# Attention scores in 64-row tiles of TensorE: two passes on opposite halves of the array

## What is computed

```python
q, k, v = split(x @ Wqkv.T + bqkv)              # 16 heads of 16
scores = einsum('bhqd,bhkd->bhqk', q, k) * hd ** -0.5
scores = where(causal, -inf, scores)            # query sees keys up to itself
attn = softmax(scores)
out = einsum('bhqk,bhkd->bhqd', attn, v)
```

## Time and profile before

| | before |
|---|---|
| median of the runs | 489.26 us |
| profiled execution, span | 490.0 us |
| TensorE busy | 400.7 us (82%) |
| VectorE busy | 327.5 us (67%) |
| ScalarE busy | 224.3 us (46%) |
| GpSimd busy | 233.4 us (48%) |
| granted TensorE clock, mean | 0.956 of full |

### The profile page before, as it was taken

How to read it: one execution, slowest core, us unless ns; L and a number is a source line. 1 busy time by engine, 2 the same in 40 slices (tenths; PEclk the granted TensorE clock), 3 DMA queues, 4 the chain that set the end, 5 groups by cost and what they waited for, 6 DMA issues and landing times.

```text
span 490.0 us, 8489 instructions
## 1 busy us (share of the span) xinstructions
PE 400.7 (82%) x2960; PEld 227.4 (46%) x2960; DVE 327.5 (67%) x619; ACT 224.3 (46%) x385; POOL 233.4 (48%) x267
## 2 busy tenths in 40 slices
PE   3737779899988999789987893887368999999980
PEld 3214335444554465443435351545145666666650
DVE  3779899558969878995688369968544444444540
ACT  2512325676556757476854761664522222232220
POOL 1482843653258622762258336347430545565542
PEclk9979999999999999899998999899859999999996
DMA  8464155726600663111222111609491344332320
GB/s 268 153 161 85 51 107 121 254 81 174 157 0 10 160 151 98 43 49 34 86 88 88 44 35 57 209 13 351 155 288 58 64 76 85 60 52 40 55 30 0
DMA packets 41319, 50.12 MB, mean 102 GB/s; under 512 B 5336, under 2 KB 36444, under 8 KB 41280
## 3 DMA queue, kind: packets, MB, share of 16 engines
q1 hardware_dynamic: 36096, 42.34, 30.3%
q0 software_dynamic: 5184, 7.25, 7.3%
HBM read 33.75 MB, written 16.75 MB: 103 GB/s over the span
## 4 chain that ended last, share of the span: by engine, by line
PE 48%; DVE 16%; POOL 7%; ACT 6%; issue 6%; DMA 5%; another core or an unknown queue 2%; SPq 0%; DVEq 0%; POOLq 0%; ACTq 0%
PE bank L1340 27%; PE bank L1454 5%; PE bank L1438 5%; PE bank L1410 3%; DVE W L1114 3%; DVE mx L1025 2%; DVE x_sb L1069 2%; PE bank L1671 2%; DMA out<-h2T,row 2%; POOL W L660 2%; ACT W L812 1%; ACT W L859 1%; PE bank L1412 1%; DVE W L1067 1%
## 5 line engine op out<-in xcount | busy, mean ns | idle before, releaser
L812 ACT ACTIVATE W<-bank 128x512 f32<-128x512 f32 (+1 forms) x176 | 95.0, 563 | 63.5 <-PE bank L1438 62.0
L1025 DVE TENSOR_REDUCE mx<-bank 128x1 f32<-128x384 f32 (+3 forms) x176 | 104.9, 633 | 23.1 <-PE bank L1412 22.6
L1340 PE MATMUL bank<-W 128*128 128x256 f16 (+2 forms) x756 | 107.4, 295 | 12.6 <-POOL W L654 3.3
L1340 PEld LDWEIGHTS bank<-W 128*128 128x128 f16 x756 | 73.9, 100 | 46.4 <-issue 12.4
L679 POOL TENSOR_SCALAR_AFFINE_SELECT W<-W 128x512 f32<-128x512 f32 x64 | 43.8, 687 | 83.3 <-ACT W L812 83.3
L1410 PE MATMUL bank<-W 126*128 126x128 f16 (+3 forms) x256 | 64.8, 308 | 14.5 <-DMA W<-qk_d 7.7
L1340 PE MATMUL bank<-W,h2T 128*128 x276 | 68.4, 385 | 3.3 <-DVE h2T L1297 2.6
L756 POOL DMA_INDIRECT out<-h2T,row x23 | 36.4, 1582 | 60.1 <-DVE h2T L1309 29.7
L1438 PE MATMUL bank<-W 128*128 128x512 f16 (+3 forms) x256 | 62.4, 305 | 2.7 <-ACT W L812 2.0
L1454 PE MATMUL bank<-W 128*32 128x128 f32 (+3 forms) x512 | 47.6, 445 | 3.1 <-POOL W L679 3.1
L1340 PE MATMUL bank<-h2T,W 128*128 128x512 f16 x192 | 44.6, 385 | 5.2 <-DVE W L1129 5.2
(11 more groups left out here) (154 smaller groups left out, 558.3 us busy)
## 6 DMA issues: line engine op xcount, KB each, us to landing
stage<-in_gup SPq DMA_DIRECT2D x14, 512.0 KB
qk_d<-W SPq DMA_DIRECT2D x48, 128.0 KB
W<-qk_d SPq DMA_DIRECT2D x32, 192.0 KB, 4.6
stage<-in_down SPq DMA_DIRECT2D x7, 512.0 KB
row<-xs_d SPq DMA_DIRECT2D x23, 130.0 KB, 5.2
xs_d<-fillb SPq DMA_DIRECT2D x2, 1040.0 KB, 5.2
x_sb<-in_x SPq DMA_DIRECT2D x4, 512.0 KB, 9.0
out<-x_sb SPq DMA_DIRECT2D x4, 512.0 KB, 4.4
```

The lines of the kernel that those rows point to most:

```text
L812: a.activation(PT[j][:, i:i + m, :], t_bank(N)[:, 0:m * w].rearrange("p (i n) -> p i n", i=m), ACT.Exp).then_inc(s_exp, 1)
L1025: v.tensor_reduce(mx_v[:, b % 2, hp0 // 4, par, i:i + m, t], SB[N % 3][:, 0:m * w].rearrange("p (i n) -> p i n", i=m), AX.X, ALU.max).then ...
L1340: i = t_.matmul(outp, l, r, start=(n == 0), stop=(n == len(prods) - 1), **kw)
```

## The change

- `scores` works on the heads of the other parity (`other_heads`), so that in each pair of units the second pass is on one half of the partitions and the first pass on the other.
- Matmuls of both passes contract only the partitions of their head: 48 rows (64 times parity onwards) in the first pass, 50 in the second. `qs` needs no second column range and no zeros; the memsets of L604 and L1167 go, and the semaphore that told of them is renamed.
- The rows of the maxima stand at partitions 48 and 49, and 112 and 113.
- The mask becomes two matmuls over 64 rows, 64 key columns of each head at a time, with selection matrices `pick` and a 64-column `maskb`. Row 63 of `maskb` masks everything, and `pick` sends it to the queries of the upper half. The columns in sum are the same.
- `constants` builds these with 18 more GpSimd instructions, most of them waiting for the one before.

```diff
+def other_heads(g):
+    return 1 - g % 2, 4 * (g // 2)

-            qs.append(early(NH * S, F16).rearrange("p (h two n) -> p h two n", two=2, n=S))
+            qs.append(early(NH // 2 * S, F16).rearrange("p (h n) -> p h n", n=S))
+            at[0] += NH // 2 * S

 def stacks(b, f):
-                if b == 0 and f == 0:
-                    sp.wait_ge(s_zero, 1)
-                if b == 1 and f == 0:
-                    sp.wait_ge(s_const, 4)
-                    sp.wait_ge(s_zero, 2)
+                if b < 2 and f == 0:
+                    sp.wait_ge(s_ones, b + 1)
-                    for a, dst in ((0, qs[r][:, :, par]), (1, ks[r])):
+                    for a, dst in ((0, qs[r]), (1, ks[r])):

 def maxima(b, f):
-                    sp.dma_start(qs[r][P - 2:P, 4 * f:4 * f + 4, par], src[par]).then_inc(s_ng[r][f], 16)
+                    p0 = 64 * par + 3 * HD
+                    sp.dma_start(qs[r][p0:p0 + 2, 4 * f:4 * f + 4], src[par]).then_inc(s_ng[r][f], 16)

 def constants():
-                link(g.tensor_copy(identb[:, :], ident[:, :]))
-                link(g.memset(maskb[:, :], 0.0))
-                g.affine_select(out=maskb[:, :], ...).then_inc(s_const, 1)
+                link(g.memset(pick[:, :, :], 0.0))
+                for lo in (0, P // 2):
+                    rows = slice(lo, lo + P // 2)
+                    link(g.memset(maskb[rows, :], 0.0))
+                    link(g.affine_select(out=maskb[rows, :], ... fill=NEG, base=0, pattern=[[-1, P // 2]], ...))
+                    link(g.affine_select(out=maskb[rows, :], ... fill=NEG, base=-(P // 2 - 1), pattern=[[0, P // 2]], ...))
+                    for part, half in ((0, 0), (1, 0), (1, 1)):
+                        link(g.affine_select(out=sel, ... fill=1.0, base=0, pattern=[[-1, P // 2]], ...))
+                    for part, half, value in ((0, 0, 0.0), (1, 0, 1.0), (1, 1, 0.0)):
+                        link(g.affine_select(out=sel, ... fill=value, base=-(P // 2 - 1), ...))
+                g.tensor_copy(ve1[0:1, 0:1], ve1[0:1, 0:1]).then_inc(s_const, 1)
...
-                g.memset(qs[1].rearrange("p h two n -> p (h two n)").bitcast(F32), 0.0).then_inc(s_const, 1)

 VectorE, before its loop
-            v.memset(qs[0].rearrange("p h two n -> p (h two n)").bitcast(F32), 0.0)

 def maxima(N) on VectorE, and def scores(N)
-                par, hp0 = group_heads(gr)
+                par, hp0 = other_heads(gr)

 def scores(N)
-                    t_.matmul(bk[:, w * i:w * (i + 1)], qs[r][0:P - 2, hp, par, P * t:w],
-                              ks[r][0:P - 2, hp, 0:w], start=(i == 0), stop=False, ...)
-                t_.matmul(bk[...][:, :, w - P:w], identb[:, :], maskb[...], start=False, stop=True, ...)
+                    p0 = 64 * par
+                    t_.matmul(bk[:, w * i:w * (i + 1)], qs[r][p0:p0 + 3 * HD, hp, P * t:w],
+                              ks[r][p0:p0 + 3 * HD, hp, 0:w], start=(i == 0), stop=False, ...)
+                rows = slice(64 * par, 64 * par + 64)
+                for part in range(2):
+                    c = w - P + 64 * part
+                    q = t_.matmul(bk[...][:, :, c:c + 64], pick[rows, part, :], maskb[rows, :]...,
+                                  start=False, stop=(part == 1), ...)

 def scores_t(N)
-                    q = t_.matmul(..., ks[r][:, hp, P * j:P * (j + 1)], qs[r][:, hp, par, P * j:S], ...)
+                    rows = slice(64 * par, 64 * par + 3 * HD + 2)
+                    q = t_.matmul(..., ks[r][rows, hp, P * j:P * (j + 1)], qs[r][rows, hp, P * j:S], ...)
```

More of the change, by code:

```diff
@@ L260, in build @@
         s_col = sem("s_col")
-        s_zero = sem("s_zero")
+        s_ones = sem("s_ones")
         s_mp = sem("s_mp")
@@ L593, in constants @@
             def constants():
-                link(g.tensor_copy(identb[:, :], ident[:, :]))
-                link(g.memset(maskb[:, :], 0.0))
-                g.affine_select(out=maskb[:, :], in_=maskb[:, :], compare_op=ALU.is_ge, fill=NEG,
-                                base=0, pattern=[[-1, P]], channel_multiplier=1).then_inc(s_const, 1)
+                link(g.memset(pick[:, :, :], 0.0))
+                for lo in (0, P // 2):
+                    rows = slice(lo, lo + P // 2)
+                    link(g.memset(maskb[rows, :], 0.0))
+                    link(g.affine_select(out=maskb[rows, :], in_=maskb[rows, :], compare_op=ALU.is_ge, fill=NEG,
+                                         base=0, pattern=[[-1, P // 2]], channel_multiplier=1))
+                    link(g.affine_select(out=maskb[rows, :], in_=maskb[rows, :], compare_op=ALU.not_equal, fill=NEG,
+                                         base=-(P // 2 - 1), pattern=[[0, P // 2]], channel_multiplier=1))
+                    for part, half in ((0, 0), (1, 0), (1, 1)):
+                        sel = pick[rows, part, 64 * half:64 * half + 64]
+                        link(g.affine_select(out=sel, in_=sel, compare_op=ALU.not_equal, fill=1.0,
+                                             base=0, pattern=[[-1, P // 2]], channel_multiplier=1))
+                    for part, half, value in ((0, 0, 0.0), (1, 0, 1.0), (1, 1, 0.0)):
+                        sel = pick[rows, part, 64 * half:64 * half + 64]
+                        link(g.affine_select(out=sel, in_=sel, compare_op=ALU.not_equal, fill=value,
+                                             base=-(P // 2 - 1), pattern=[[0, P // 2]], channel_multiplier=1))
+                g.tensor_copy(ve1[0:1, 0:1], ve1[0:1, 0:1]).then_inc(s_const, 1)
                 po.wait_ge(s_const, 2)
@@ L1409, in scores @@
                     hp = hp0 + i0 + i
-                    t_.matmul(bk[:, w * i:w * (i + 1)], qs[r][0:P - 2, hp, par, P * t:w],
-                              ks[r][0:P - 2, hp, 0:w], start=(i == 0), stop=False, skip_group_check=True)
-                t_.matmul(bk[:, 0:m * w].rearrange("p (i n) -> p i n", i=m)[:, :, w - P:w], identb[:, :],
-                          maskb[:, :].unsqueeze(1).to_broadcast([P, m, P]), start=False, stop=True,
-                          skip_group_check=True).then_inc(s_s1, 1)
+                    p0 = 64 * par
+                    t_.matmul(bk[:, w * i:w * (i + 1)], qs[r][p0:p0 + 3 * HD, hp, P * t:w],
+                              ks[r][p0:p0 + 3 * HD, hp, 0:w], start=(i == 0), stop=False, skip_group_check=True)
+                rows = slice(64 * par, 64 * par + 64)
+                for part in range(2):
+                    c = w - P + 64 * part
+                    q = t_.matmul(bk[:, 0:m * w].rearrange("p (i n) -> p i n", i=m)[:, :, c:c + 64],
+                                  pick[rows, part, :], maskb[rows, :].unsqueeze(1).to_broadcast([64, m, 64]),
+                                  start=False, stop=(part == 1), skip_group_check=True)
+                q.then_inc(s_s1, 1)
             def max_turn(b, f):
@@ L1437, in scores_t @@
                     hp = hp0 + i0 + i
-                    q = t_.matmul(t_bank(N)[:, w * i:w * (i + 1)], ks[r][:, hp, P * j:P * (j + 1)],
-                                  qs[r][:, hp, par, P * j:S], start=True, stop=True)
+                    rows = slice(64 * par, 64 * par + 3 * HD + 2)
+                    q = t_.matmul(t_bank(N)[:, w * i:w * (i + 1)], ks[r][rows, hp, P * j:P * (j + 1)],
+                                  qs[r][rows, hp, P * j:S], start=True, stop=True)
                 q.then_inc(s_st, 1)
```

13 lines of the change are left out of this document (6 added, 7 removed).

## The result

| | before | after |
|---|---|---|
| median of 16 runs each | 489.13 us | 499.86 us |
| lowest and highest | 487.86, 490.90 | 489.36, 506.72 |
| profiled execution, span | 490.0 us | 498.1 us |
| granted TensorE clock, mean of it | 0.956 | 0.900 |

The medians of all 16 runs lie 10.7 us or 2.2% apart. The ratio of undisturbed runs alone (those within 1.5% of the kernel's fastest, 6 of the 16 after, with a median of 492.9 us) is 1.0066, with a 95% interval of 1.0044 to 1.0087. So the loss is some 3 us in the quickest runs and nearer 11 in the middle of the spread, where the profiled execution lies. The forecast was 482, with a range to 496.

The account below looks back on a forecast made before the run. TensorE was taken to bound stage 0, with VectorE next and close in stages 1 and 2. Gains of 4.5, 1.7 and 2.3 us less 1.1 lost make 7.4: 490.0 to 482.6, forecast 482, range 475 to 496.

Parts of the forecast that it names:

- Overlap works: Both passes, stages 0 to 2: array halves work at once, a group takes 3.03 us, not 5.18, before deductions.
- 0.29 us a group: Taken off the overlap's 2.15 us because first-pass units start only with the last second-pass matmul ahead; leaves 1.86 us.
- no overlap: Rival: the halves don't run at once but the switches of form are paid; 494.7 us, chance 0.20.
- slow loads: Rival: loads of 64-row weights aren't hidden, 5.3 us a group, all of the gain; 495 to 500 us, chance 0.08.
- Changes of form: TensorE, between full-form jobs and the passes' row tiles: 129 more changes at 0.09 us, 11.7 us raw over all stages.
- Stage -1: First pass alone: VectorE sets the stage's length, so TensorE's 1.6 us of switches cost only 0.1 us.
- Stage 0: 7.1 us saved by overlap, less 1.8 of switches, is 5.3; 4.5 after VectorE and ScalarE take some.
- the next engine holds the pace: Rival: only stage 0 gains, 4.5 us less 1.1 and some wait; 486 to 488 us, chance 0.16.
- Stage 1: Overlap saves 2.9 us on the chain, less 1.2 of switches: 1.7 us gained.
- Stage 2: 5.0 us saved less 1.3 of switches is 3.7; cut to 2.3 since VectorE has only 5.3 us idle.
- Stage 3: No second lane to overlap; 40% of 2.6 us of switches, 1.0 us lost.
- The last sentence of the prediction: A fall of the granted clock in a stage that had 1.00 or 0.97 would make the forecast wrong; no chance given.

Follow-up runs that it names:

- twins on the other half: Changed kernel with stage -1 score matmuls (but the last few) issued again on the idle half, result unused, then mask matmuls too: 500.27 us, then 499.99 us.
- the doubles: Late-mask hybrid with every second-pass matmul of stages 0 to 2 issued twice into the same bank: 497.99 us, ratio 1.0188.
- late-mask hybrid: Changed kernel with half rows only in stages 0 to 2, GpSimd's selection instructions moved to the end of stage -1: median 496.28 us.
- clean hybrid: Changed kernel with half rows only in stages 0 to 2, GpSimd's selection instructions split over two idle gaps: 493.98 us, ratio 1.0049.

## Why the prediction was wrong

7.4 us were to be gained, and 10.7 were lost between the medians. Three steps of the sum failed. It kept the granted clock of the kernel before in every stage, a term put at nothing; it took TensorE's slack in stage -1 for cover; and in stage 0 it left out GpSimd's queue. By its parts:

- **Overlap works** (its main step): right, down to the 0.01 us between the halves; the pair takes 0.24 us where 0.25 to 0.30 were forecast. Too cautious was only the 0.29 us a group taken off because a first-pass unit would start with the last matmul of the unit ahead: it starts with the first (110.93 against 111.05). The rivals "no overlap" and "slow loads" fall with it, though the time after (499.9) is what the second had given at its upper end; that is chance.
- **Changes of form, 0.09 us each, 4.3 us on the chain in stages 0 to 2**: right. 0.09 and 0.10 in the timeline, 5.0 us (3.0 to 7.2) in the run that had them alone, with 70 of the 82. (The Trainium skill, TensorEngine Tiling (Array Packing), "Tiling Modes", Key Properties, has a change of mode drain the engine; the trace agrees in that each change to or from 64-row tiles costs 0.09 or 0.10 us.)
- **Stage -1, "VectorE-bound, 0.1 lost"**: wrong, 4.5 lost. The step took TensorE's slack for cover (26.8 of 35.9 us busy) and counted columns and changes only. But the work on half rows left the clock at 0.67, TensorE became busy 36.7 of 40.4 us, and the cover was gone. Shown by twins on the other half (37.9, then 36.8 us); with all rows in this stage it is 35.7. Nor was the stage VectorE's before: its chain (first, 36.1 to 72 us) has next to nothing of TensorE, and after (34 to 80 us) TensorE's L1354, L1425 and L1430 are most of it.

```profile
by line: DMA ng_d<-negm 14.7%; ACT W L787 8.1%; POOL W L660 7.6%; DMA qk_d<-W 7.6%; DVE mx L1025 5.1%; SPq L467 4.6%; DMA W<-ng_d 4.3%; DVE W L980 3.9%; PE bank L1372 3.7%; DVE W L992 3.7%; POOL W L654 3.2%; POOL h2T L640 3.0%; POOL h2T L63
```
```profile
by line: PE bank L1354 29.7%; PE bank L1425 25.4%; DMA W<-qk_d 11.3%; PE bank L1430 10.4%; DVE mx L1040 7.2%; ACT W L816 5.9%; PE bank L1386 3.9%; issue 3.6%; ACT W L802 3.2%; PE bank L1458 3.1%; DVE W L1007 1.7%; PE bank L1437 1.4%; ACT W 
```

- **Stage 0, 4.5 gained**: wrong, nothing gained at a clock of 0.91 to 0.96. I had allowed 0.8 us for VectorE and ScalarE "three units behind at most" and left out GpSimd's queue, where 2.8 us of additions stand ahead of a mask. With them gone, and the clock at 1.00, the gain is 2.8 us (46.8 to 44.0), still short of 4.5. This is the rival "the next engine holds the pace", but in the stage that it had left alone.
- **Stage 1, 1.7 gained**: wrong, 3.7 lost. The sum had the clock stay at 1.00; it falls at the stage's end, and stays low. TensorE's timeline at the edge, where GpSimd's mask ended its wait:

```profile
171.66 0.43 PE L1474 MATMUL bank<-W 128*32 128x128 f32 x8 [2.21 <-POOL W L694]
```

In windows around the fall, after:

```profile
163.00:173.40 10.40, 8.07 (x93) 3.83 (x91) 9.49 (x18) 7.78 (x17) 8.59 (x11) 1.00 0.58 142
173.40:190.50 17.10, 17.10 (x137) 8.56 (x135) 8.64 (x19) 7.07 (x13) 2.54 (x4) 0.50 0.64 157
190.50:200.00 9.50, 8.90 (x100) 5.14 (x95) 8.33 (x17) 6.29 (x12) 2.68 (x3) 1.00 0.28 95
```

and around the fall that the kernel before has in stage 2:

```profile
197.00:205.00 8.00, 5.45 (x52) 2.89 (x49) 7.90 (x19) 3.32 (x6) 5.98 (x9) 1.00 0.23 66
205.00:208.40 3.40, 3.40 (x16) 2.08 (x15) 3.37 (x9) 1.37 (x4) 2.86 (x5) 0.50 0.00 0
208.40:215.00 6.60, 5.37 (x50) 2.15 (x48) 6.57 (x13) 4.72 (x10) 5.47 (x7) 1.00 0.05 3
```

Before, TensorE was idle 2.6 of 8 us, fell to 1.2 GHz, and was back after 3.4 us of full work on all rows. After, it was idle 2.3 of 10.4 us, fell, and worked without a gap for 17.1 us at 1.2 GHz before the clock came back; counted from one matmul's start to the next, 6.4 of the 17.1 us went to half rows and 10.6 to other matmuls, so these windows alone don't put the length down to half rows. The fall has an idle stretch ahead of it in both; its length is what is new. The other traces bear that out: in stage 1 all seven with all rows have 1.00, and those with half rows and overlap 0.86 to 0.97 (1.00 only with the doubles); falls that begin in stages 0 to 2 last 3.4 or 6.8 us where the stage has all rows, and 3.4 to 20.5 us with half rows and overlap. By the clock that it had in each trace, with half rows and overlap and without doubles:

| | us at granted clock |
|---|---|
| stage 1 (55.5 at 1.00 before) | 56.2 at 0.97; 56.9 at 0.94; 58.0 to 59.2 at 0.92; 59.0, 59.1 at 0.89; 60.6 at 0.86 |
| stage 2 (50.6 at 0.97 before) | 48.8, 48.8, 49.7 at 0.90; 51.4 at 0.87; 51.7 to 52.3 at 0.86; 54.6 at 0.81 |

So most of the 3.7 us goes with the clock, but at 0.97 (in the late-mask hybrid, behind its longer stage 0) stage 1 is still 0.7 us longer than before: the gain of 1.7 isn't there either. Changes of form alone gave 56.8 us, so overlap brought about 0.6 us there for the 2.9 in the sum. What took the rest stays open.
- **Stage 2, 2.3 gained**: wrong in this kernel, 1.6 lost, with the clock at 0.86 from that same stretch (to 190.5) and one at 214.4. The gain does exist: 1.8 us in the stage in two traces where the clock was 0.90; the kernel with half rows in this stage alone is probably faster than before, by 0.4% between medians.
- **Stage 3, 1.0 lost**: 0.7, right.
- **The last sentence of the prediction**, that a fall of the granted clock would make it wrong, named the cause; but it had no price and no chance. The earlier trace rows had the clock at 0.98 and 0.97 in three stages, so it did fall there, with TensorE busy 26.8 of 35.9 us in stage -1: a change that halves the rows at work wanted its own rival.

**What stays open.** In stage -1 the gradient is shown. In stages 1 and 2 it isn't settled what starts a fall, nor what makes it long: without overlap stage 1 kept 1.00 with half rows (more of the time busy: 53.8 of 57.2 us), stage 2 did not (60.3 of 62.8). That overlap leaves TensorE more idle, and half rows make falls long, would fit most of the traces, but not that stage 2, and it isn't shown. That the clock is what the 16 runs differ by is a correlation; which way it goes isn't shown, since a stretched stall would lower it too.

Of the kernels with the full output the one with half rows in stage 2 alone is the lowest, 488.65 us. Without the output bias additions on GpSimd the clean hybrid is at 486.46, but the kernel before without them is at 487.32, so like for like half rows bring about 0.9 us (1.8 by the ratios, 0.9943 against 0.9980). To move the additions to an idle place is the next thing to try, and wasn't tried.

## What to carry to other kernels

Zero rows in a matmul are not only waste: before taking them away, look at the granted clock and at how busy TensorE is in each stage, and give the fall to 1.2 GHz a price and a chance, above all in a stage where nothing else runs in the rows that are freed. Use row tiles where two lanes run side by side and full-form jobs are few, stage by stage, not everywhere. And before a gain on the bounding engine is put in the sum, walk through every other engine's queue in that stage, item by item, for what the old bound had hidden.
